# A mixture-of-experts gate on VectorE: each expert ranked by two wide comparisons and a triangle, in place of pairs

## The reference, cut to what matters

```python
def _moe(h, w_gate, we1, be1, we2, be2):          # E = 4 experts, TOP_K = 2
    raw = jax.nn.softmax(x @ w_gate, axis=-1)
    top_vals, top_idx = jax.lax.top_k(raw, TOP_K)
    w = jax.nn.softmax(top_vals, axis=-1)
    comb = jnp.zeros((t, E), x.dtype).at[jnp.arange(t)[:, None], top_idx].add(w)
    hmid = jax.nn.gelu(jnp.einsum('td,edi->tei', x, we1) + be1[None], approximate=False)
    eout = jnp.einsum('tei,eid->ted', hmid, we2) + be2[None]
    out = jnp.einsum('te,ted->td', comb, eout)
```

## Time and profile before

| | |
|---|---|
| median of 3 runs | 1252.61 us (1251.7 to 1254.48) |
| profiled execution, its own time | 1252.02 us |
| its span in the trace | 1250.2 us |
| mean granted clock of TensorE | 0.985 |
| busy: PE, DVE, ACT, POOL | 1145.9, 983.0, 657.0, 668.0 us |
| instructions on DVE | 2299 |

### The profile page before, as it was taken

One profiled execution on the slowest core, in us unless ns is written; L12 is line 12 of the kernel. 1 busy time (PEld: TensorE's weight loads), 2 busy tenths in 40 slices (PEclk: granted clock), 3 DMA queues, 4 the chain that ended last, 5 costly groups with the idle time before them and its releaser, 6 DMA issues.

```text
span 1250.2 us, 29573 instructions
## 1 busy us (share of the span) xinstructions
PE 1145.9 (92%) x11172; PEld 937.1 (75%) x11172; DVE 983.0 (79%) x2299; ACT 657.0 (53%) x1685; POOL 668.0 (53%) x715
## 2 busy tenths in 40 slices
PE   4799899799999999878999999999999999997997
PEld 4576676566676666555899889988999888886786
DVE  2667686788888888977888688877887778957887
ACT  3465564375766667565555444444445344466563
POOL 6666564545545455253777554545445444446565
PEclk9899999999999999989999999999999999999999
DMA  8664443333343333302121000000000100001110
GB/s 216 163 154 117 106 120 87 85 89 100 99 106 100 95 102 90 109 18 77 60 68 52 1 1 1 1 2 1 1 2 1 34 2 21 15 3 39 30 39 30
DMA packets 98142, 76.21 MB, mean 61 GB/s; under 512 B 73387, under 2 KB 86315, under 8 KB 98001
## 3 DMA queue, kind: packets, MB, share of 16 engines
q1 hardware_dynamic: 98001, 74.33, 22.2%
HBM read 53.40 MB, written 19.92 MB: 59 GB/s over the span
## 4 chain that ended last, share of the span: by engine, by line
PE 58%; DVE 19%; issue 8%; POOL 6%; ACT 5%; DMA 2%; SPq 2%; DVEq 0%; POOLq 0%; ACTq 0%
PE bank L1414 4%; PE bank L512 4%; PE bank L1415 4%; PE bank L1416 4%; PE bank L1470 4%; PE bank L1443 4%; DVE B_nr L637 4%; DVE PT L646 3%; PE bank L448 3%; PE bank L375 3%; PE bank L455 2%; PE bank L490 2%; PE bank L1430 2%; PE bank L1432 2%; PE bank L1431 2%
## 5 line engine op out<-in xcount | busy, mean ns | idle before, releaser
L1711 POOL TENSOR_TENSOR C_QK<-C_t1b,C_t2b 128x512 f32<-128x512 f32 x128 | 166.8, 1303 | 247.3 <-DVE C_t2b L1555 247.2
L1552 DVE SCALAR_TENSOR_TENSOR C_t1b<-bank,C_bcol,C_tabs 64x512 f32<-64x512 f32 x256 | 192.0, 750 | 53.3 <-PE bank L1416 49.1
L637 DVE TENSOR_REDUCE B_nr<-bank 128x4 f32<-128x512 f32 x256 | 164.4, 684 | 36.8 <-PE bank L455 35.5
L1414 PE MATMUL bank<-C_XTh,C_Wh 128*128 128x512 f32 x256 | 112.4, 439 | 5.4 <-POOL C_XTl L1403 3.7
L863 ACT ACTIVATE PT<-bank 128x512 f32<-128x512 f32 x160 | 91.9, 597 | 47.5 <-PE bank L490 47.2
L1663 ACT ACTIVATE C_V<-bank 128x512 f32<-128x512 f32 x64 | 38.1, 598 | 147.8 <-PE bank L1432 146.1
L858 ACT ACTIVATE PT<-PT 128x512 f32<-128x512 f32 x96 | 59.5, 631 | 93.4 <-DVE PT L646 93.4
L1644 ACT ACTIVATE C_P<-bank,C_nm 128x128 f32<-128x128 f32 x256 | 90.7, 367 | 31.6 <-DVE C_nm L1565 30.0
L1415 PE MATMUL bank<-C_XTl,C_Wh 128*128 128x512 f32 x256 | 101.3, 396 | 0.0
L1416 PE MATMUL bank<-C_XTh,C_Wl 128*128 128x512 f32 x256 | 101.3, 396 | 0.0
L512 PE MATMUL bank<-PT,vpool 128*32 128x128 f32 x2048 | 97.5, 286 | 3.2 <-ACT PT L858 3.1
(11 more groups left out here) (256 smaller groups left out, 3657.0 us busy)
## 6 DMA issues: line engine op xcount, KB each, us to landing
Adrq<-PB SPq DMA_DIRECT2D x16, 192.0 KB, 2.8
stk<-Adrq SPq DMA_DIRECT2D x16, 192.0 KB
Adrk<-PB SPq DMA_DIRECT2D x16, 192.0 KB, 2.7
stk<-Adrk SPq DMA_DIRECT2D x16, 192.0 KB
Bdrq<-PB SPq DMA_DIRECT2D x16, 192.0 KB, 2.9
stk<-Bdrq SPq DMA_DIRECT2D x32, 96.0 KB
Bdrk<-PB SPq DMA_DIRECT2D x16, 192.0 KB, 2.8
stk<-Bdrk SPq DMA_DIRECT2D x32, 96.0 KB
```

The source lines that it names most:

```text
L637: e.tensor_reduce(dst, bank[n % 2][:, :].rearrange("p (a b) -> p a b", a=4), AX.X, ALU.max, negate=True).then_inc(sem("m_dve"), 1)
L1414: e.matmul(o[:, :], CWh[hp][:, cs], XCh[0][:, t, :], start=t == 0, stop=False)
L1552: e.scalar_tensor_tensor(out=v4(t1b[kq][lo:lo + 64, :]), in0=v4(o[hi:hi + 64, :]), scalar=bc[hi:hi + 64, :], in1=tabsC[hi:hi + 64, 2 * kq ...
L1711: e.tensor_tensor(QK[v % 3][:, kq, :], t1b[kq][:, :], t2b[kq][:, :], ALU.add).then_inc(sem("rc_pool"), 1)
```

## The change

The ranking of part 1 becomes five instructions on 4 x 4 x 4 = 64 numbers per partition (row, expert, rival): all rivals greater than the expert, all rivals equal to it, the second multiplied by a triangle that keeps only rivals with a lower number, the sum of both, and its sum over the rivals. The triangle is a table of 128 x 16 numbers, one more input, loaded behind the biases. The gate has 18 DVE instructions in place of 28, and all counts of `gate_dve` follow. `C_pad` goes; the triangle's tile stands on the other stack, ahead of C's tiles.

```diff
-    PAD = 16
+    lower = sb("D_lower", [128, 4, 4], F32, st_d)
-    sb("C_pad", [128, PAD], F32, st_c)
-    ge = sb("D_ge", [128, 6, 4], F32, st_d)
-    gl = sb("D_gl", [128, 6, 4], F32, st_d)
+    ahead = sb("D_ahead", [128, 4, 4, 4], F32, st_d)
+    equal = sb("D_equal", [128, 4, 4, 4], F32, st_d)
...
+        e.dma_start(lower[:, :, :], I["c_lower"]).then_inc(sem("ld_D"), 16)
...
-        q.wait_ge("ld_D", 32)
+        q.wait_ge("ld_D", 48)
...
-            for k, (a, b) in enumerate(pairs):
-                e.tensor_tensor(ge[:, k, :], pr[:, :, a], pr[:, :, b], ALU.is_ge).then_inc(sem("gate_dve"), 1)
-            q.wait_ge("gate_dve", n + 12)
-            e.tensor_scalar(gl[:, :, :], ge[:, :, :], -1.0, 1.0, ALU.mult, ALU.add).then_inc(sem("gate_dve"), 1)
-            q.wait_ge("gate_dve", n + 13)
-            for x in range(4):
-                terms = [ge[:, k, :] for k, (a, b) in enumerate(pairs) if b == x] + [gl[:, k, :] for k, (a, b) in enumerate(pairs) if a == x]
-                e.tensor_tensor(cnt[:, :, x], terms[0], terms[1], ALU.add).then_inc(sem("gate_dve"), 1)
-                q.wait_ge("gate_dve", n + 14 + 2 * x)
-                e.tensor_tensor(cnt[:, :, x], cnt[:, :, x], terms[2], ALU.add).then_inc(sem("gate_dve"), 1)
-            q.wait_ge("gate_dve", n + 21)
+            rival, own = pr[:, :, :].unsqueeze(2).to_broadcast([128, 4, 4, 4]), pr[:, :, :].unsqueeze(3).to_broadcast([128, 4, 4, 4])
+            e.tensor_tensor(ahead[:, :, :, :], rival, own, ALU.is_gt).then_inc(sem("gate_dve"), 1)
+            e.tensor_tensor(equal[:, :, :, :], rival, own, ALU.is_equal).then_inc(sem("gate_dve"), 1)
+            q.wait_ge("gate_dve", n + 8)
+            q.wait_ge("ld_D", 48)
+            e.tensor_tensor(equal[:, :, :, :], equal[:, :, :, :], lower[:, :, :].unsqueeze(1).to_broadcast([128, 4, 4, 4]),
+                            ALU.mult).then_inc(sem("gate_dve"), 1)
+            q.wait_ge("gate_dve", n + 9)
+            e.tensor_tensor(ahead[:, :, :, :], ahead[:, :, :, :], equal[:, :, :, :], ALU.add).then_inc(sem("gate_dve"), 1)
+            q.wait_ge("gate_dve", n + 10)
+            e.tensor_reduce(cnt[:, :, :], ahead[:, :, :, :], AX.X, ALU.add).then_inc(sem("gate_dve"), 1)
+            q.wait_ge("gate_dve", n + 11)
             e.tensor_scalar(sel[:, :, :], cnt[:, :, :], 2.0, None, ALU.is_lt).then_inc(sem("gate_dve"), 1)
...
+    c["c_lower"] = np.broadcast_to(np.tril(np.ones((4, 4), f), -1), (128, 4, 4)).copy()
```

More of the change, by code:

```diff
@@ L1809, in program @@
             if m == 1:
-                dtakes(("gate", c), ("gate_dve", 28 * c + 1))
+                dtakes(("gate", c), ("gate_dve", 18 * c + 1))
             if m == 0:
@@ L1850, in comb_t_pe @@
     def comb_t_pe(e, q, c):
-        q.wait_ge("gate_dve", 28 * (c + 1))
+        q.wait_ge("gate_dve", 18 * (c + 1))
         o = dturn_bank(q, ("ct", c))
@@ L1904, in gate_dve @@
     def gate_dve(e, q, c, part):
-        n = 28 * c
+        n = 18 * c
         bc = lambda a: a.unsqueeze(2).to_broadcast([128, 4, 4])
-        pairs = [(a, b) for a in range(4) for b in range(a + 1, 4)]
         if part == 0:
@@ L1923, in gate_dve @@
             q.wait_ge("gate_dve", n + 6)
-            for k, (a, b) in enumerate(pairs):
-                e.tensor_tensor(ge[:, k, :], pr[:, :, a], pr[:, :, b], ALU.is_ge).then_inc(sem("gate_dve"), 1)
-            q.wait_ge("gate_dve", n + 12)
-            e.tensor_scalar(gl[:, :, :], ge[:, :, :], -1.0, 1.0, ALU.mult, ALU.add).then_inc(sem("gate_dve"), 1)
-            q.wait_ge("gate_dve", n + 13)
-            for x in range(4):
-                terms = [ge[:, k, :] for k, (a, b) in enumerate(pairs) if b == x] + [gl[:, k, :] for k, (a, b) in enumerate(pairs) if a == x]
-                e.tensor_tensor(cnt[:, :, x], terms[0], terms[1], ALU.add).then_inc(sem("gate_dve"), 1)
-                q.wait_ge("gate_dve", n + 14 + 2 * x)
-                e.tensor_tensor(cnt[:, :, x], cnt[:, :, x], terms[2], ALU.add).then_inc(sem("gate_dve"), 1)
-            q.wait_ge("gate_dve", n + 21)
+            rival, own = pr[:, :, :].unsqueeze(2).to_broadcast([128, 4, 4, 4]), pr[:, :, :].unsqueeze(3).to_broadcast([128, 4, 4, 4])
[10 more added lines that the diff above has]
+            q.wait_ge("gate_dve", n + 11)
             e.tensor_scalar(sel[:, :, :], cnt[:, :, :], 2.0, None, ALU.is_lt).then_inc(sem("gate_dve"), 1)
             e.tensor_reduce(mx[:, :], pr[:, :, :], AX.X, ALU.max).then_inc(sem("gate_dve"), 1)
-            q.wait_ge("gate_dve", n + 23)
+            q.wait_ge("gate_dve", n + 13)
             e.tensor_tensor(pr[:, :, :], pr[:, :, :], bc(mx[:, :]), ALU.subtract).then_inc(sem("gate_dve"), 1)
@@ L1941, in gate_dve @@
             e.tensor_tensor(ew[:, :, :], ew[:, :, :], sel[:, :, :], ALU.mult).then_inc(sem("gate_dve"), 1)
-            q.wait_ge("gate_dve", n + 25)
+            q.wait_ge("gate_dve", n + 15)
             e.tensor_reduce(mx[:, :], ew[:, :, :], AX.X, ALU.add).then_inc(sem("gate_dve"), 1)
-            q.wait_ge("gate_dve", n + 26)
+            q.wait_ge("gate_dve", n + 16)
             e.reciprocal(mx[:, :], mx[:, :]).then_inc(sem("gate_dve"), 1)
-            q.wait_ge("gate_dve", n + 27)
+            q.wait_ge("gate_dve", n + 17)
             e.tensor_tensor(comb[c % 2][:, :, :], ew[:, :, :], bc(mx[:, :]), ALU.mult).then_inc(sem("gate_dve"), 1)
@@ L2011, in gate_act @@
         if k == 0:
-            q.wait_ge("gate_dve", 28 * c + 3)
+            q.wait_ge("gate_dve", 18 * c + 3)
             e.activation(pex[:, :, :], lg[:, :, :], ACT.Exp).then_inc(sem("gate_act"), 1)
         else:
-            q.wait_ge("gate_dve", 28 * c + 24)
+            q.wait_ge("gate_dve", 18 * c + 14)
             e.activation(ew[:, :, :], pr[:, :, :], ACT.Exp).then_inc(sem("gate_act"), 1)
```

## The result

| | before | after |
|---|---|---|
| median of 8 runs, side by side | 1253.93 us | 1250.88 us (1248.66 to 1251.69) |
| ratio | | 0.9967, 95% interval [0.9958, 0.9976] |
| profiled execution, own time | 1252.02 us | 1250.70 us |
| its span; TensorE's mean granted clock | 1250.2 us; 0.985 | 1248.9 us; 0.979 |
| busy: PE, DVE, ACT, POOL | 1145.9, 983.0, 657.0, 668.0 us | 1150.0, 980.1, 656.4, 667.1 us |

The kernel is faster by 0.33%, 4.1 us [3.0, 5.3], by the ratio of the runs; 3.8 was forecast. The two medians alone differ by 3.05 us, the low end of that interval. Medians and ratios are those of the ordinary runs: in experiment 9 one execution (2004 us), and one of the kernel before beside it (1561 us), fell in a slower state and are left out.

What follows compares the result with a forecast made beforehand. DVE was taken to be late in a chunk's first half, PE full in its second. Gains 1.25 + 1.3 + 0.64 + 0.60 = 3.8 us gave 1252.0 - 3.8 = 1248.2, or 1248.8 against the median; range 1247.0 to 1251.6.

Steps and rivals of the forecast that it cites:

- Which wait counts: Gate on DVE: a two-input instruction meeting a running POOL instruction waits until it is done; POOL's train's end counts.
- Prices of the new ones: Gate on DVE, without POOL's interference: a wide comparison takes 0.23 us, the reduction 0.22 us.
- 0.7 us for each wide comparison: Gate: a wide comparison's cost if every four broadcast rows cost anew; part of the little-done rival, chance 0.08.
- Chunk 0: 1.25: Chunk 0's gate, five POOL instructions in the way: part 1 ends 1.25 us earlier and everybody gets it.
- Chunk 1: 1.3: Chunk 1's gate, four POOL subtractions beside it: part 1 ends 1.3 us earlier, and all 1.3 arrives.
- the second slips through behind it as the old second did: Chunk 1's gate: the second wide comparison isn't held by POOL, so the product waits out POOL's second, the sum its third.
- the stated lower bound, 0.95: Chunk 1's gain in us if the second comparison is held as well and the sum meets POOL's fourth.
- Chunk 2: 0.64 of it arrives: Chunk 2: DVE gains as in chunk 1, but PE bounds; 0.64 us at its transpose arrives, the other 0.7 is lost.
- Chunk 3: 0.60: Chunk 3, only two POOL instructions: DVE gains 0.8 us, PE gets its 0.60 us wait, and 0.60 arrives.
- PE's waits: PE's waits for D_comb: the first falls from 2.96 to 1.7 us, the others (0.67, 0.64, 0.60) to near nothing.
- The clock: Slower rival: TensorE's clock falling in PE's own stretch costs 1.7 us each time, decisive from three times; chance 0.07.
- The time before 1108 moves by over 1 us: Sign that the prediction is wrong: time before 1108 us, where no gate runs, moving by over 1 us.

Runs made afterwards that it cites:

- experiment 9: Kernel before, its six pair comparisons kept, with only POOL's D_X moved from behind the sixth piece to behind the eighth: 1253.99 us, 0.9996 of the kernel before.
- Experiments 4: Changed kernel, but the ranking's first comparison waits for the last D_HL of POOL's row of subtractions: 1258.36 us, 1.0034 of the kernel before.
- 5: Changed kernel with the product by the triangle done twice in each gate: 1251.01 us, 0.9973 of the kernel before.
- 6: Changed kernel with seven narrow comparisons in place of the wide ones, product and sum gone, reduction kept: 1249.68 us, 0.9957 of the kernel before.
- experiment 3: Changed kernel without its five ranking instructions, D_sel taken from a fixed threshold: 1247.13 us, 0.9940 of the kernel before.
- Experiment 7: Changed kernel with POOL's residual D_X moved two pieces later, to the end of the chunk's list: 1247.66 us, 0.9942 of the kernel before.
- experiment 1: Kernel before with its pairs, plus the changed kernel's table, DMA, missing pad and tile addresses: 1256.04 us against 1254.33, ratio 1.001.
- 2: Changed kernel with wide comparisons only in chunk 0's gate, pairs in chunks 1 to 3: 1253.49 us against 1254.33, 0.9992 of the kernel before.
- its repetition: The changed kernel with D_X two pieces later, run again beside the pairs with D_X later: 1246.35 us, 0.9935 of the kernel before.

## Why the prediction was right, and where not

- **Which wait counts.** Held for this change: part 1 ends behind POOL's train, and only what stands after the train's last instruction is gained. Experiments 4, 5 and 6 each show it; experiment 3 shows that a row with few enough instructions gets out of the train before its end.
- **Prices of the new ones.** 0.23 and 0.22 us forecast, 0.22 and 0.22 measured. The "0.7 us for each wide comparison" never came.
- **Chunk 0: 1.25.** Measured 1.32 in part 1 and 1.38 at the first D_y. Five were held, as forecast; D_sel was (0.95) and the reduction wasn't. ACT's table load, 1131.56 to 1132.84, was over 0.1 us before the subtraction ended, so little more was to be had.
- **Chunk 1: 1.3.** Measured 1.03, and 1.0 at the next D_y (1.38 to 2.37). This is the term that was mis-sized. The step that failed is "the second slips through behind it as the old second did": it was held (1.33 us), the sum met POOL's fourth, and the gate came out near the stated lower bound, 0.95.
- **Chunk 2: 0.64 of it arrives.** DVE gained 0.93 in the gate, all of it there at the next D_y (3.30). It was not cut to 0.64, on DVE or on PE: PE began the next gate's logits at 1201.18 in place of 1203.22, 3.3 us ahead by the same count, though its wait at the transpose only went from 0.64 to 0.57. So the wait at the transpose was the wrong measure of what PE can take. Behind it the fall of the clock hides what PE would have kept, 3.3 ahead before it and 1.8 after.
- **Chunk 3: 0.60.** Part 1 gained 1.0 (4.45 to 3.45) where 0.8 was forecast; ahead from 1.77 at its start to 2.6 at the end, 0.8.
- **PE's waits.** The first came down to 1.65 (1.7 forecast). The others were to be "near nothing" and are 0.59, 0.57 and 0 us: D_comb is caught by POOL's D_X, which comes as much earlier as DVE does. Experiment 7 removes just that.
- **The clock.** I gave the falls uncovered 1.7 us each; one came in the profiled execution, for 1.5. The median clock of the changed kernel's runs is 0.979, and that of before is 0.979 to 0.980 in the three later sessions (beside the changed kernel its clocks weren't recorded), so nothing shows that it weighed on the comparison. Among the runs of the changed kernel those at 0.982 took 1248.66 and 1249.1 us, those at 0.979 1250.7 to 1251.69. As a rival for this change it did not win; in experiment 9 it was as large as anything the edit could have given.
- **The sum.** 3.8 forecast, 4.1 [3.0, 5.3] measured, 3.05 by the medians. The median itself, 1250.88, is 2.1 above the 1248.8 of the forecast: 1.3 of it because before's own median, run beside the changed kernel, was 1253.93 and not 1252.61, and 0.75 because the medians show less gain than 3.8. In the profiled pair, 2.6 from the first comparison on, and with the fall's 1.5 given back 4.1; that so small a difference fits is luck with two errors, 0.3 too much for chunk 1 and 0.5 too little for chunks 2 and 3.
- **"The time before 1108 moves by over 1 us" was to be a sign against me.** It moved by 1.28 us. Layout explains none of it: at the same addresses the first comparison came at 1124.49 in experiment 1 and at 1124.52 in 2, with the wide ranking at 1126.76 in 7 and at 1124.16 in its repetition. One kernel differs from itself by 2.6 us there, and it lost 20 us of clock before 600 us the first time and 15 in the repetition. So the sign pointed at the clock of parts A and B, not at the change, and a threshold of 1 us was too narrow.

The best kernel run is the wide ranking with D_X later: 0.9942 and 0.9935 of before in two sessions.

## What to carry to other kernels

Where DVE works beside a POOL engine that is full, price a row of small instructions by what stands behind POOL's last one, and not by the number or the durations in the trace. Here taking instructions out of the train gave nothing as long as DVE was still held at its end, and taking them from behind it gave part 1 all of their time; only when nearly the whole row went (experiment 3) did DVE leave the train early. How much of that reaches the end depends on the next engine: of 14.7 us less in the gates 3.4 arrived. Then look for the next small instruction that meets a long one of POOL; here moving one POOL instruction by two places gave the wide kernel another 0.25 to 0.3% by the medians, and the pairs nothing that could be seen. And when PE is near its limit, read the clock in every profile, both in its full stretch and far ahead of the change, before you credit an edit: two falls more or less outweigh a microsecond's edit.

## What the runs showed of the hardware that was not expected

- A free narrow comparison (128x4) starts 0.08 us behind the one before and slipped through behind a held one; a wide one (128x64) starts 0.14 us behind (1217.11, 1217.25) and was caught each time in chunks 0, 1 and 2 (1.32 and 1.33 us). So the same kind of instruction may pass or not between two of POOL's; whether it is the size or the distance of the starts wasn't told apart.
- A held instruction lasts 1.2 us for 0.2 us of work, a tensor-scalar of 16 elements with one input too (0.95 and 1.04, and 1.17 in experiment 3); a reduction (0.22 us) and the statistics (0.39 us) passed.
- TensorE's clock fell to its lower level in places that moved from kernel to kernel and between two executions of one kernel. Most falls took 1.5 to 1.7 us of PE's work; experiments 1 and 4 each had a long one, between 1130 and 1155 us, that took some 7 us.
